# Second token pair: seven narrow products in place of whole tails, with operands made one pair earlier

## What is computed

```python
h = x @ W.T + 2 * sum_e gates1[e] * (x @ A[e].T) @ B[e].T   # 8 experts of rank 16, best two kept, softmax of the two
y = h @ Wf.T + bf + sum_e 2 * softmax(h @ Wrf.T)[e] * (h @ Af[e].T) @ Bm[e]   # 4 experts of rank 8
out = x + y
```

## Time and profile before

| | |
|---|---|
| median of 3 runs | 323.65 us (323.32 to 323.68) |
| span of the profiled execution, first to last instruction | 321.9 us |
| own time of the profiled execution | not listed apart from its span |
| PE busy | 318.2 us, 99% of the span |
| PEld busy | 311.9 us, 97% |
| DVE busy | 262.5 us, 82% |
| ACT busy | 128.2 us, 40% |
| POOL busy | 11.3 us, 3%, 13 instructions |
| granted TensorE clock | 1.000 throughout |
| first pair, from its tails | 99.29 to 127.69 us |
| second pair | 127.69 to 156.15 us |
| third pair | 156.15 to 183.23 us |

### The profile page before, as it was taken

One profiled execution on the slowest core, in us unless ns is written; L12 is line 12 of the kernel. 1 busy time (PEld: TensorE's weight loads), 2 busy tenths in 40 slices (PEclk: granted clock), 3 DMA queues, 4 the chain that ended last, 5 costly groups with the idle time before them and its releaser, 6 DMA issues.

```text
span 321.9 us, 5996 instructions
## 1 busy us (share of the span) xinstructions
PE 318.2 (99%) x2246; PEld 311.9 (97%) x2246; DVE 262.5 (82%) x609; ACT 128.2 (40%) x258; POOL 11.3 (3%) x13
## 2 busy tenths in 40 slices
PE   8999999999999999999999999999999999999996
PEld 5999999999999899899999999999999999999996
DVE  3999999798799778988968968878895987888543
ACT  3872836495147236325412503421251350333111
POOL 1001003700000000000000000000000000000000
DMA  7999000000000312700330150051025006002003
GB/s 266 419 404 290 3 2 0 2 0 2 0 2 0 132 24 46 260 3 0 109 154 1 60 201 0 0 191 70 0 74 187 0 21 239 0 0 110 24 0 130
DMA packets 10704, 27.59 MB, mean 86 GB/s; under 512 B 3166, under 2 KB 4702, under 8 KB 10688
## 3 DMA queue, kind: packets, MB, share of 16 engines
q1 hardware_dynamic: 10256, 26.83, 23.5%
q10 hardware_dynamic: 432, 0.53, 0.5%
HBM read 18.97 MB, written 8.39 MB: 85 GB/s over the span
## 4 chain that ended last, share of the span: by engine, by line
PE 98%; DMA 1%; DVE 0%; issue 0%
PE sums L1310 98%; DMA in<-part 1%; PE sums L1571 0%; DVE rows L1069 0%; DVE b_high L806 0%
## 5 line engine op out<-in xcount | busy, mean ns | idle before, releaser
L1310 PE MATMUL sums<-b_high,a_high 128*128 128x256 f32 (+1 forms) x224 | 45.3, 286 | 0.3 <-DVE b_high L806 0.3
L1310 PE MATMUL sums<-b_low,a_high 128*128 128x256 f32 (+1 forms) x224 | 45.2, 286 | 0.0
L1310 PE MATMUL sums<-b_high,a_low 128*128 128x256 f32 (+1 forms) x224 | 45.0, 286 | 0.0
L1310 PEld LDWEIGHTS sums<-b_high,a_high 128*128 128x128 f32 x224 | 34.7, 189 | 1.0 <-ACT a_high L549 0.8
L1310 PEld LDWEIGHTS sums<-b_low,a_high 128*128 128x128 f32 x224 | 34.7, 189 | 0.0
L1310 PEld LDWEIGHTS sums<-b_high,a_low 128*128 128x128 f32 x224 | 34.6, 188 | 0.0
L1310 PE MATMUL sums<-t_high,s_high 128*128 128x354 f32 x96 | 31.3, 326 | 0.0
L1310 PE MATMUL sums<-t_low,s_high 128*128 128x354 f32 x96 | 31.1, 324 | 0.0
L1310 PE MATMUL sums<-t_high,s_low 128*128 128x354 f32 x96 | 31.1, 324 | 0.0
L1069 DVE TENSOR_TENSOR rows<-sums,rows 128x354 f32<-128x354 f32 x48 | 24.4, 522 | 4.1 <-PE sums L1310 3.4
L1310 PE MATMUL sums<-ct_low,st_high 128*128 128x244 f32 (+1 forms) x80 | 25.6, 320 | 0.0
(11 more groups left out here) (151 smaller groups left out, 845.8 us busy)
## 6 DMA issues: line engine op xcount, KB each, us to landing
stage<-tokens SPq DMA_DIRECT2D x14, 512.0 KB, 4.0
out<-rows SPq DMA_DIRECT2D x14, 512.0 KB, 4.9
in<-part SPq DMA_DIRECT2D x7, 585.0 KB, 8.8
in<-part SPq DMA_DIRECT2D x4, 777.0 KB, 14.0
in<-part SPq DMA_DIRECT2D x4, 265.0 KB, 16.4
rows<-tokens SPq DMA_DIRECT2D x2, 512.0 KB, 13.6
out<-rows SPq DMA_DIRECT2D x3, 192.0 KB, 2.3
c_plain<-gate_proj SPq DMA_DIRECT2D x1, 544.0 KB, 18.0
```

Of the source, the lines that this page charges most:

```text
L1310: return nc.tensor.matmul(out_, lhs, rhs, start=start, stop=stop, skip_group_check=True)
```

## The change

Three things are changed, all around the second pair (j = 1).

1. PE: the second pair starts with the wide products 1 and 6. Then come the seven narrow products, then the rest as in the pairs behind it, with product 5 cut after its first chunk to take the transposes of u. The 48 matmuls of 488 columns go.
2. The narrow parts of T1, T3 and T2 are made on DVE in the first pair and rounded for T2 and T3 there on ACT; T4 is made in the second pair. The blocks that they are made in are others (`TN_PLACE`), and the order of rounding is T2, T3, T1, T4. S1 to S4 of the second pair are made earlier in the first.
3. The low part of the second pair's tokens is no longer `split_x` on DVE. ACT writes the negated rounding of the tokens into `st_low` (`negate_x`), and POOL issues a transfer that adds the tokens from HBM to it. `load_pair(2)` now waits for that negation and is issued ahead of the loop.

The diff, cut to its core:

```diff
-        TN_ORDER = (T1, T3, T2, T4)
+        TN_PLACE = {T1: C11, T2: C22, T3: C12, T4: C21}
+        TN_ORDER = (T2, T3, T1, T4)
@@ SP
-            def load_pair(j):
+            def load_pair(j, splits=None):
                 sp.wait_ge(s_made, 4 * j)
                 for odd in range(2):
-                    sp.wait_ge(x_split[odd], j)
+                    if splits is None:
+                        sp.wait_ge(x_negated[odd], 1)
+                    else:
+                        sp.wait_ge(x_split[odd], splits)
                     sp.dma_start(stage[:, odd, :], tokens[2 * j + odd]).then_inc(x_here[odd], 16)
...
-            with sp.Fori(0, PAIRS - 2) as j:
-                load_pair(j + 2)
+            load_pair(2)
+            store(0)
+            with sp.Fori(1, PAIRS - 2) as j:
+                load_pair(j + 2, j + 2)
                 store(j)
@@ POOL
+            for odd in range(2):
+                pool.wait_ge(x_negated[odd], 1)
+                pool.dma_start(st_low[:, odd, :, :].rearrange("p k c -> p (k c)"), tokens[2 + odd],
+                               accum_op=ALU.add).then_inc(x_added[odd], 16)
@@ ACT
+            def negate_x(odd):
+                nc.scalar.activation(st_low[:, odd, :, :].rearrange("p k c -> p (k c)"), stage[:, odd, :], ACT.Copy,
+                                     scale=-1.0).then_inc(x_negated[odd], 1)
...
-                steady = not first and not second
+                steady = not first
...
-                if second:
-                    round_tn(T1, t1n_made)
-                    round_tn(T3, t3n_made)
-                    act.wait_ge(narrow_ready, 2)
-                    round_tn(T2, t2n_made)
+                if second:
+                    round_tn(T1, t1n_made)
                 if steady:
                     act.wait_ge(tails_out, j)
-                    act.wait_ge(p1n_done, j - 1)
+                    act.wait_ge(p1n_done, j)
                     copy(narrow[:, 1, 0, :], narrow_bank(BANK_NA)).then_inc(r1n_read, 1)
-                    act.wait_ge(p2n_done, j - 1)
+                    act.wait_ge(p2n_done, j)
                     copy(narrow[:, 0, 0, :], narrow_bank(BANK_NA)).then_inc(n11_out, 1)
+                if second:
+                    round_tn(T4, t4n_made)
+                    act.wait_ge(stored[1], 16 * j)
+                    copy(rows[:, 1, wide_at(0)], bank(BANK_A)).then_inc(r1_read, 1)
...
-                if not steady:
+                if first:
                     act.wait_ge(p2_done, j + 1)
                     round_x(j + 1, 0)
+                    negate_x(0)
...
+                if first:
+                    round_next(j + 1, S2, p6_done)
+                if not last:
                     round_next(j + 1, S3, p7_done)
...
                 copy(rows[:, 0, wide_at(0)], bank(BANK_A)).then_inc(a_out, 1)
                 if first:
-                    round_next(j + 1, S2, p6_done)
-                    round_next(j + 1, S3, p7_done)
+                    next_odd()
+                    negate_x(1)
+                    act.wait_ge(narrow_ready, 1)
+                    round_tn(T2, t2n_made)
+                    round_tn(T3, t3n_made)
                 if not last:
                     round_next(j + 1, S1, p5_done)
@@ DVE, pair
+                if second:
+                    split_tn(T3)
+                if steady:
+                    split_s(j, S1)
+                if second:
+                    split_tn(T1)
+                if steady:
+                    dve.wait_ge(r1n_read, j)
+                    dve.wait_ge(p6n_done, j)
+                    add_sums(narrow[:, 0, 1, :], narrow_bank(BANK_NB), narrow[:, 1, 0, :]).then_inc(u2n_read, 1)
+                if second:
+                    dve.wait_ge(t2n_made, 1)
+                    make_tn(C21, C21, C22, t4n_made)
+                if steady:
+                    split_s(j, S4)
+                    dve.wait_ge(p7n_done, j)
                     add_sums(narrow[:, 1, 1, :], narrow_bank(BANK_NB), narrow[:, 1, 0, :]).then_inc(u3n_read, 1)
+                if second:
+                    split_tn(T4)
...
                     next_s(S3)
+                    if second:
+                        add_u2()
...
-                if not steady:
+                if first:
                     add_r22()
-                if second:
-                    split_tn(T4)
-                if not last:
+                    next_s(S4)
+                    split_s(j + 1, S2)
+                    dve.wait_ge(gate_again, 64)
+                    make_tn(C11, C12, C11, t1n_made)
+                elif not last:
                     split_x(j + 1, 0)
...
                 if first:
-                    split_s(j + 1, S2)
+                    make_tn(C12, C22, C12, t3n_made)
+                    dve.wait_ge(t1n_made, 1)
+                    make_tn(C22, C22, C11, t2n_made)
                     split_s(j + 1, S3)
                 dve.wait_ge(c_done, j + 1)
                 add_sums(rows[:, 0, wide_at(1)], bank(BANK_C), rows[:, 0, wide_at(1)]).then_inc(c_out, 1)
+                if first:
+                    split_tn(T2)
@@ PE, pair
+                if second:
+                    pe.wait_ge(x_added[0], 16)
+                    pe.wait_ge(a_out, j)
+                    product_1(j)
+                    product_6(j)
                 if steady:
-                    narrow_products(j)
+                    narrow_products(j, second)
...
-                else:
-                    pe.wait_ge(tails_out, j)
-                    pe.wait_ge(x_split[0], j + 1)
-                    tail(0, range(KC))
-                    pe.wait_ge(x_split[1], j + 1)
-                    tail(1, range(KC)).then_inc(narrow_ready, 1)
...
                 of_s(BANK_B, S3, t_high[T3], t_low[T3], False).then_inc(p7_done, 1)
+                if second:
+                    pe.wait_ge(s_split, 4 * j + S_NO[S1])
+                    pe.wait_ge(c_out, j)
+                    of_s(BANK_C, S1, t_high[T1], t_low[T1], True, range(1))
+                    turn_u()
+                    of_s(BANK_C, S1, t_high[T1], t_low[T1], False, range(1, HALF)).then_inc(p5_done, 1)
```

More of the change, by code:

```diff
@@ L719, in pair @@
                 ins.then_inc(pair_exp_ready, 1)
[L721 to L724, removed]
+                if not second:
+                    if not first:
+                        act.wait_ge(stored[1], 16 * j)
+                    act.wait_ge(p1_done, j + 1)
+                    copy(rows[:, 1, wide_at(0)], bank(BANK_A)).then_inc(r1_read, 1)
                 if first:
@@ L734, in pair @@
                     round_x(j + 1, 0)
-                if steady and not last:
+                turning = steady and not second and not last
+                if turning:
                     act.wait_ge(u_half_turned, j - 1)
@@ L1085, in pair @@
             def pair(j, first=False, second=False, last=False):
-                steady = not first and not second
-                turning = steady and not last
+                steady = not first
+                turning = steady and not second and not last
                 base = STEPS * j
@@ L1100, in next_s, with add_u2 @@
                         add_s(j + 1, n, s_plain)
[L1102 to L1110, removed]
-                if second:
[L1113 to L1118, removed]
+                def add_u2():
+                    if not first:
+                        dve.wait_ge(stored[0], 16 * j)
+                    dve.wait_ge(r1_read, j + 1)
+                    dve.wait_ge(p6_done, j + 1)
+                    add_sums(rows[:, 0, wide_at(1)], bank(BANK_B), rows[:, 1, wide_at(0)]).then_inc(u2_read, 1)
@@ L1142, in pair @@
+                    dve.wait_ge(n12_out, j)
                     gate_logits = narrow[:, :, :, GH - E1 // 2:GH]
@@ L1196, in add_r22 @@
                     add_sums(rows[:, 1, wide_at(1)], bank(BANK_C), rows[:, 1, wide_at(1)]).then_inc(r22_read, 1)
[L1199 to L1203, removed]
+                if not second:
+                    add_u2()
+                if first:
+                    next_s(S1)
                 if turning:
@@ L1239, in pair @@
                                         negate=True).then_inc(neg_max_ready, 1)
+                if first:
+                    next_s(S2)
                 if second or turning:
@@ L1258, in pair @@
                 ins.then_inc(v_turned, 1)
-                if turning:
+                if first:
+                    next_s(S3)
+                if turning or second:
                     split_s(j + 1, S2)
@@ L1431, in tail, with wide @@
                 return last
-            def wide(n, a_high, a_low, a_at, b_high, b_low, fresh):
-                for k in range(HALF):
+            def wide(n, a_high, a_low, a_at, b_high, b_low, fresh, chunks=range(HALF)):
+                for k in chunks:
                     for kind in (HH, HL, LH):
@@ L1601, in pair @@
                 lora(BANK_A, 0, 0)
-                if second or last:
+                if last:
```

(2 more changed lines are left out.)

114 lines of the change are left out of this document (56 added, 58 removed).

## The result

| | before | after |
|---|---|---|
| median | 323.62 us (323.27 to 323.75, 6 runs) | 324.53 us (324.07 to 325.28, 6 runs) |
| ratio, 95% interval | | 1.0034 (1.0023 to 1.0044) |
| profiled execution, its span | span 321.9 | 324.6, span 323.3 |
| second pair, from where its first matmul follows the one ahead to the third pair's first | 28.46 (127.69 to 156.15) | 28.59 (127.65 to 156.24) |
| last addition on DVE | 319.31 to 319.84 | 319.61 to 320.14 |

The change makes the kernel slower: by 0.91 us between the medians, and by 0.34%, which is 1.1 us, as the ratio estimates it. The forecast was 0.40 faster. The table already shows that most of the loss doesn't lie in the second pair: 1.1 us come behind the last addition of the whole kernel.

A forecast was written before the change was run, and what follows sets the result against it. TensorE was taken to bound the kernel, busy 318.2 of 321.9 us. The terms -1.12 + 0.50 + 0.21 + 0 = -0.41 us, added to the median 323.65, gave 323.24, said as 323.25; range 322.5 to 325.6.

The forecast's parts named there:

- the first adding transfer: Before the second pair's first product: lands at 127.5, 5.4 us after the negation, needed by 127.54; stall 0.
- the end of the program: No term: the sum was a difference inside the span, and the 1.75 us outside first and last instruction stay.
- TensorE's work: Second pair: 48 matmuls of 488 columns removed (10.65 us), 84 of 244 added (9.53 us); -1.12 us.
- T4, +0.50: Second pair, after product 5: T4's split ready at 138.74, TensorE restarts at 138.89 instead of 138.39; stall 0.50 us.
- Transposing u, +0.21: Second pair: u plus restart takes 4.60 us after the narrow columns, TensorE's covering work 4.39; stall 0.21 us.
- The moved DVE and ACT steps: Steps moved into the first pair fit in idle time or finish before TensorE needs them, some narrowly; no cost.
- rival C: First add late, ahead of second pair's product 1: each us over 5.4 adds one; 324.6 to 325.8 us; chance 0.33.
- The rival by which POOL's issue starves beside a busy DVE: POOL takes 8.88 us to issue the first add, which lands 6.9 to 7.9 late: about 330.5 us; chance 0.06.

The follow-up runs named there:

- The version without waits: Changed kernel with third token tile rounded early, twenty idle instructions on DVE, T4 made and rounded earlier, T1 split later: 322.27 us, 0.9976 against the kernel before.
- the last two versions: Changed kernel with third token tile rounded early and twenty idle DVE instructions, 322.74 us; the same with T4 made earlier and T1 split later, 322.27 us.

## Why the prediction was wrong

Two terms failed: the first adding transfer, put at a stall of 0, and the end of the program, which the sum leaves out. Either alone would have turned the forecast gain into a loss. The measured 324.53 lies inside the stated range, 322.5 to 325.6, but by luck: the range reaches that far for an adding transfer 1.4 to 2.6 us late; it was 0.8 late, and the rest comes from a step that no rival has.

1. **TensorE's work, -1.12:** right. The version without waits takes 1.11.
2. **T4, +0.50:** right, mechanism and size (0.50 in the changed kernel's starts, 0.49 between the last two versions). DVE added product 7's bank at 137.97 and split T4 from 138.30 to 139.47, where the text has 0.21, 0.33 and 1.17 behind product 7. PE restarted only 0.05 behind that, not 0.15, but took 0.11 more for the product.
3. **Transposing u, +0.21:** no wait. u was complete at 146.66, 4.32 behind the narrow columns in place of 4.45, and PE came at 146.73, 4.39 behind them, which is its own work alone. It came 0.07 behind u, so 0.15 was too much for that, too. Without this term the sum would have been -0.62.
4. **The moved DVE and ACT steps, nothing:** right. The splits of T2, T3 and T1 began at 130.83, 131.92 and 133.69, and no wait of PE names them, also where PE came on time.
5. **The first adding transfer, 0:** this term was mis-sized. The text made it 3.4 + 0.65 + 1.36 = 5.4 from the negation; it took 6.2 and cost 0.78. The plain part was nearly right: 0.3 from the negation to the issue and 3.9 for a plain transfer from POOL make 4.2, against 4.05. What failed is the 1.36 for the destination, read at the rate of plain transfers: adding made 2.0 of it (5.9 less 3.9; over all profiles 1.4 to 2.0). And the estimate, 127.5, was set against a need at 127.54, with no room for either. This is rival C in place and rule (one for one), with a smaller lateness than the 1.4 to 2.6 us that C was given.
6. **The end, not in the sum:** the larger part of the miss. "My sum is a difference inside the span" took it, without a reason given, that what follows TensorE's last work is the same in both kernels. It isn't: +1.1 us in the trace, 0.9 on the median. The text never asked where the lists' lengths place the instruction fetches.

The Trainium skill, "Runtime: NRT & Kernel Launch", Instruction fetch mechanics, says that each engine's sequencer fetches its instructions over DMA in 16 KiB blocks, and that the cost is mostly hidden. For most of them the trace agrees: of 19 fetches in the span of the changed kernel no wait of PE shows one. It also shows when one isn't hidden: with packets of the last store behind it, 0.9 to 1.2 us. The blocks on queue q14, the late one among them, are of 8 KB here and not of 16; there the measurement decides.

By the sum: inside the span up to the third pair +0.13, in place of -0.41. The third pair adds 0.19, a wait that the forecast doesn't have, and the tail 1.1, which makes 1.4, as the profiled spans say (321.9 and 323.3). The runs show 0.91 between the medians and 1.1 by the ratio; single profiles differ by some tenths in the later pairs.

What stays open: which instruction of DVE's list triggers the extra fetch, and by how many instructions it could be moved before it returns (only 11 more on the kernel before, and 20 more on the changed one, were tried); how the DMA engine with the fetch is chosen; and what makes ut_low late in the third pair.

## What to carry to other kernels

Price a transfer from its issue, by the longest comparable landing, and have its source ready that much earlier: here one ACT step in another order was worth 0.8 us of pair time. Look at what follows the last compute instruction as at a stage of its own, before and after; a difference there that no operand explains may be an instruction fetch beside the last store, and some idle instructions, or fewer of them, move it. When one new wait is moved, look at once at what stands behind the moved step: T4 helped only when T1 gave way too.

## What the runs showed of the hardware

- An edit in the second pair can cost 1 us at the end of the program through the length of one engine's instruction list alone: 11 more instructions on DVE, with the kernel before, tail 2.0 to 3.1; 20 more, with the changed kernel, tail 3.1 to 2.0. Three on ACT, 76 on PE and seven on SP did nothing there.
- A transfer with an add of 512 KB lands 5.3 to 5.9 us after its issue by POOL with little else moving, a plain one 3.9; a packet of 4 KB takes 0.40 us in the one and 0.19 in the other. Beside a load the second add took 5.5 to 10.0. In the changed kernel, while only the adding transfer moved, the rate was low and the DMA engines busy; stretch, busy times, clock, DMA share, GB/s:

```profile
124.00:125.00 1.00, 1.00 (x8) 1.00 (x7) 1.00 (x3) 0.65 (x2) 0.00 (x0) 1.00 0.87 82
125.00:126.00 1.00, 1.00 (x8) 1.00 (x7) 1.00 (x2) 1.00 (x3) 0.00 (x0) 1.00 0.83 139
```

- The rival by which POOL's issue starves beside a busy DVE didn't come: 1.03 and 0.86 us, while DVE had hardly a gap.
- Instructions that only wait aren't free on TensorE: 76 of them kept it idle 8.3 us in place of 0.3, 0.11 each, and behind that idle time the granted clock of the stretch from 10 to 20 us was 0.63 on average, between its levels of 1.2 GHz (0.5) and 2.4 GHz, where the kernel before shows 1.00:

```profile
10.00:20.00 10.00, 7.71 (x44) 7.75 (x45) 6.46 (x13) 6.07 (x14) 0.00 (x0) 0.63 1.02 420
```
